# The running maximum of an mLSTM goes to all partitions by transfers instead of matmuls, and the order of a pass is changed

## The reference

```python
def mlstm(q, k, v):                      # one sequence, 8 heads of 64
    ig, fg = gates(concat(q, k, v))      # (8, 256) each
    cs = cumsum(log_sigmoid(fg))
    log_D = where(tril, cs[s] - cs[t] + ig[t], -inf)
    m = max(log_D, axis=t)
    C = (q @ k.T / 8) * exp(log_D - m)
    h = C / (max(|sum C|, exp(-m)) + 1e-6) @ v
    return layernorm(h) * ln_scale
x = x + tanh(g0) * mlstm(layernorm(x), ctx, ctx)
z = layernorm(x)
x = x + tanh(g1) * (top2_of_16_experts(z) + shared_expert(z))
```

## Time and the profile before

| what | value |
|---|---|
| median of three runs | 1074.41 us (1070.31 to 1075.37) |
| the profiled execution | 1070.1 us, of which 1068.5 us are the span from the first to the last instruction |
| busy share of the span | PE 90%, PEld 75%, DVE 76%, ACT 40%, POOL 39% |
| mean granted clock of TensorE | 0.956 of full speed |
| chain that ended last, by engine | PE 69%, DVE 13%, issue 7%, DMA 5%, POOL 4% |
| L1084 and L1086, all of the loop | 256 matmuls each, 48.9 and 44.7 us busy |

### The profile page before, as it was taken

One profiled execution on the slowest core, in us unless ns is written; L12 is line 12 of the kernel. 1 busy time (PEld: TensorE's weight loads), 2 busy tenths in 40 slices (PEclk: granted clock), 3 DMA queues, 4 the chain that ended last, 5 costly groups with the idle time before them and its releaser, 6 DMA issues.

```text
span 1068.5 us, 21065 instructions
## 1 busy us (share of the span) xinstructions
PE 959.1 (90%) x6143; PEld 804.3 (75%) x6143; DVE 807.3 (76%) x1995; ACT 424.7 (40%) x957; POOL 419.4 (39%) x315
## 2 busy tenths in 40 slices
PE   3689999999999998988998399999999999999982
PEld 2569888988898886977777278888888888677761
DVE  2887889888988989898866576666666666555885
ACT  2654445444544554444522134444444444332110
POOL 5010211221122122222123827668667777104775
PEclk9989999999999999999958699999999999999996
DMA  7570201220122022111004475576677674915888
GB/s 253 209 311 2 80 31 51 80 79 21 61 80 80 10 72 81 60 60 41 11 31 158 139 227 178 178 231 186 179 212 214 177 213 150 335 70 153 261 291 260
DMA packets 92778, 147.26 MB, mean 138 GB/s; under 512 B 10720, under 2 KB 51168, under 8 KB 91776
## 3 DMA queue, kind: packets, MB, share of 16 engines
q0 software_dynamic: 17872, 65.02, 18.8%
q1 hardware_dynamic: 62896, 59.79, 17.9%
q10 hardware_dynamic: 11904, 21.11, 5.6%
HBM read 89.26 MB, written 56.62 MB: 137 GB/s over the span
## 4 chain that ended last, share of the span: by engine, by line
PE 69%; DVE 13%; issue 7%; DMA 5%; POOL 4%; ACT 1%; SPq 1%; DVEq 0%; POOLq 0%; ACTq 0%
PE bank L1282 19%; PE bank L1152 13%; PE bank L1301 9%; PE bank L1165 5%; PE bank L1075 4%; POOL w_ring L699 3%; PE bank L1007 3%; PE bank L1096 2%; PE bank L1097 2%; PE bank L1349 2%; PE bank L1099 2%; DMA x2n<-routed_x 2%; PE bank L1292 2%; DMA base_out<-in_x_dram 2%; PE bank L1125 1%
## 5 line engine op out<-in xcount | busy, mean ns | idle before, releaser
L1282 PE MATMUL bank<-w_ring,x2nT 128*128 x948 | 254.3, 406 | 13.9 <-DVE x2nT L1864 13.6
L1282 PEld LDWEIGHTS bank<-w_ring,x2nT 128*128 128x128 f32 x948 | 173.8, 191 | 51.5 <-issue 15.8
L1152 PE MATMUL bank<-x2nT,w_ring 128*128 128x256 f32 x1152 | 149.8, 286 | 0.0
L580 POOL DMA_INDIRECT routed_x<-x2n,slot_u x64 | 65.8, 1029 | 204.4 <-DVE slot_u L1625 189.5
L1152 PEld LDWEIGHTS bank<-x2nT,w_ring 128*128 128x128 f32 x1152 | 142.3, 190 | 0.3
L1301 PE MATMUL bank<-w_ring,sh_actT 128*128 x474 | 121.2, 391 | 3.5 <-DVE sh_actT L1853 3.5
L1853 DVE TENSOR_TENSOR sh_actT<-bank,sh_actT 128x256 fp32r<-128x256 f32 x79 | 33.6, 425 | 108.9 <-ACT sh_actT L922 108.9
L1301 PEld LDWEIGHTS bank<-w_ring,sh_actT 128*128 128x128 f32 x474 | 88.8, 188 | 24.0 <-issue 4.6
L662 POOL TENSOR_TENSOR w_ring<-area,one 128x3072 fp32r<-128x3072 f32 x14 | 74.2, 5303 | 81.4 <-PE bank L1301 81.4
L699 POOL DMA_INDIRECT w_ring<-routed_y,y_slot x64 | 66.9, 1046 | 78.0 <-DMA routed_y<-cs_in 52.9
L665 POOL TENSOR_TENSOR w_ring<-area,w_ring 128x3072 fp32r<-128x3072 f32 x14 | 95.9, 6849 | 2.5 <-POOL w_ring L662 2.5
(11 more groups left out here) (224 smaller groups left out, 1959.1 us busy)
## 6 DMA issues: line engine op xcount, KB each, us to landing
x2n<-routed_x SPq DMA_DIRECT2D x316, 64.0 KB, 2.6
routed_y<-cs_in ACTq DMA_DIRECT2D x79, 256.0 KB, 3.3
base_out<-in_x_dram SPq DMA_DIRECT2D x16, 512.0 KB, 5.1
cs_in<-in_ctx_dram SPq DMA_DIRECT2D x16, 512.0 KB, 4.0
area<-n_L_ffn_expert_gate_dram POOLq DMA_DIRECT2D x16, 512.0 KB, 5.2
area<-in_L_ffn_expert_up_dram POOLq DMA_DIRECT2D x16, 512.0 KB, 6.9
area<-n_L_ffn_expert_down_dram POOLq DMA_DIRECT2D x16, 512.0 KB, 8.4
out_dram<-base_out SPq DMA_DIRECT2D x32, 256.0 KB, 3.8
```

The lines of the kernel that those rows point to most:

```text
L580: pool.indirect_dma_start(out=routed_x, in_=x2n[:, b.par, j, :], in_offset=None, out_offset=bass.IndirectOffsetOnAxis(ap=slot_u[:, b.par, ...
L1152: last = mm(gu_bank(b.n, m)[:, at:at + S], w[:, w_part, c, m * P:(m + 1) * P], x2nT[:, x_part, c, :], start=(c + p == 0), stop=(c == DC - ...
L1282: last = mm(bank[2 + t.par][:, :], xtT[:, x_part, t.par, c * P:(c + 1) * P], w_gu[:, bass.ds(slot, 1), w_part, c, :].rearrange("p a i -> p ...
```

## The change

- spread, its constants (identb, mask_b, head_sel), the bf16 parts of max_row and the banks MB go. Instead SP stores max_row to DRAM (max_store) and loads it back, two heads at a time, into all 128 partitions (max_load: the two rows whole, and their second halves once more). GpSimd writes the mask into the first copy (mask, one select of 128 x 512 elements for two heads). ScalarE's head reads the result from SBUF.
- max_spread has two buffers; the load of pair q waits until the decays of pair q - 2 are made.
- The banks that MB held become a second pair of score banks, so scores_pair runs one pair further ahead.
- GpSimd's order: two masks of A behind h_stats, then values, x2_stats, two masks of F, stats, and scatter last.
- VectorE: top and choose go behind turn(G, 0); rank behind turn(G, 1); stats, slots and weigh to other places behind rows_end. ScalarE: top goes behind turn(G, 0), ahead of heads 6 and 7. TensorE: rank behind turn(G, 1), scores_pair(A, 3) ahead of gates_sum.
- The zero rows are written in four pieces in steps t = 5 to 8, the kept weights in six pieces in steps t = 10 to 15.

```diff
-        TP, SM, MB, QK, HO, FF = bank[0], bank[1], bank[2:4], bank[4:6], bank[6], bank[7]
+        TP, SM, QK, HO, FF = bank[0], bank[1], (bank[4:6], bank[2:4]), bank[6], bank[7]
...
-        max_rest = sb("max_rest", [FG + NH, S])[FG:, :]
-        max_parts = sb("max_parts", [P, 2, S], BF16)
+        max_spread = sb("max_spread", [P, 2, 2 * ST + 2, P])
...
-        zeros = base_out[:, NT // 2, :]
+        zeros = base_out[:, NT - 1, :]
...
-        row_step = event("row_step", 8)
-        max_hi_made = event("max_hi_made")
+        row_step = event("row_step", 5)
+        max_out = event("max_out", 16)
+        max_in = [event(f"max_in{k}", 32) for k in range(2)]
+        max_masked = event("max_masked")
...
+            def max_store(b):
+                sp.wait_ge(row_step.sem, row_step.upto(b.n, 4))
+                sp.dma_start(max_rows[b.par], max_row[:, :]).then_inc(max_out.sem, 16)
+
+            def max_load(b, q):
+                k, lap = q % 2, b.n * 2 + q // 2
+                sp.wait_ge(max_out.sem, max_out.upto(b.n))
+                sp.wait_ge(decay_made.sem, decay_made.upto(b.n, 2 * q - 2))
+                two = max_rows[b.par, 2 * q:2 * q + 2, :]
+                sp.dma_start(max_spread[:, k, 0:2 * ST, :].rearrange("p (h j) n -> p h (j n)", h=2),
+                             two.partition_broadcast(P)).then_inc(max_in[k].sem, 16)
+                sp.dma_start(max_spread[:, k, 2 * ST:, :], two[:, P:S].partition_broadcast(P)
+                             ).then_inc(max_in[k].sem, 16)
+
+            def max_front(b):
+                max_store(b)
+                max_load(b, 0)
+                max_load(b, 1)
+
+            def max_back(b):
+                max_load(b, 2)
+                max_load(b, 3)
+
             load_next(Item(0, 2))
+            max_front(Item(0, 0))
+            max_back(Item(0, 0))
             load_next(Item(0, 3))
-            sp.wait_ge(zeros_made.sem, zeros_made.upto(0))
-            sp.dma_start(routed_x[0:DUMP, :].rearrange("(e r) d -> r e d", e=E)[0:P],
-                         zeros.unsqueeze(1).to_broadcast([P, E, D])).then_inc(padded.sem, 16)
-            sp.dma_start(routed_x[DUMP:DUMP + P, :], zeros).then_inc(padded.sem, 16)
+            max_front(Item(0, 1))
             sp.wait_ge(shared_in.sem, shared_in.upto(SHARED_PIECES - 1))
-            for part in range(2):
-                sp.dma_start(kept_w[part], sh_flat[:, part, :].bitcast(F32)).then_inc(kept_w_out.sem, 16)
+
+            def pad(k):
+                own = routed_x[0:DUMP, :].rearrange("(e r) d -> r e d", e=E)[0:P, k * PADS:(k + 1) * PADS]
+                sp.dma_start(own, zeros.unsqueeze(1).to_broadcast([P, PADS, D])).then_inc(padded.sem, 16)
+
+            def keep_w(k):
+                part, at = k // 3, slice(k % 3 * DC * IS, (k % 3 + 1) * DC * IS)
+                sp.dma_start(kept_w[part][:, at], sh_flat[:, part, at].bitcast(F32)).then_inc(kept_w_out.sem, 16)
             for b in range(4, B):
-                if b == B // 2 - 2:
-                    sp.wait_ge(padded.sem, padded.upto(1))
+                if b == B - 3:
+                    sp.wait_ge(padded.sem, padded.upto(E // PADS))
+                max_back(Item(0, b - 3))
                 load_next(Item(0, b), more=b + 2 < B)
+                if b == B // 2:
+                    sp.wait_ge(zeros_made.sem, zeros_made.upto(0))
+                    sp.dma_start(routed_x[DUMP:DUMP + P, :], zeros).then_inc(padded.sem, 16)
+                if B // 2 <= b < B // 2 + E // PADS:
+                    pad(b - B // 2)
+                max_front(Item(0, b - 2))
+                if b >= B - 3:
+                    keep_w(b - B + 3)
+            for b in range(B - 3, B):
+                max_back(Item(0, b))
+                if b + 1 < B:
+                    max_front(Item(0, b + 1))
+                keep_w(b - B + 6)
...
-                g.memset(zeros, 0.0).then_inc(zeros_made.sem, 1)
-                const(g.memset(identb[:], 0.0))
...
-                const(g.memset(mask_b[:], 0.0))
...
-                const(g.memset(max_parts[:], 0.0))
...
-                select(identb[:], 1.0, ALU.not_equal, 0, 1, [[-1, P]])
...
-                select(mask_b[:], MASK, ALU.is_ge, 0, -1, [[1, P]])
...
-                const(g.memset(head_sel[:], 0.0))
-                for part in range(3):
-                    select(head_sel[:], 1.0, ALU.not_equal, -FG * part, 1, [[-1, NH], [0, P]])
...
+            def mask(b, q):
+                k, lap = q % 2, b.n * 2 + q // 2
+                pool.wait_ge(max_in[k].sem, max_in[k].upto(lap))
+                own = max_spread[:, k, 0:2 * ST, :]
+                g.affine_select(out=own, in_=own, compare_op=ALU.is_ge, fill=MASK, base=0,
+                                pattern=[[0, 2 * ST], [1, P]], channel_multiplier=-1).then_inc(max_masked.sem, 1)
...
+                if attend:
+                    mask(A, 2)
+                    mask(A, 3)
+                if front:
+                    values(F)
                 if route:
                     x2_stats(G)
+                if front:
+                    mask(F, 0)
+                    mask(F, 1)
+                if ahead:
+                    stats(N)
                 if rest and route:
                     scatter(H)
-                if front:
-                    values(F)
-                if ahead:
-                    stats(N)
...
+                if t == 4:
+                    pool.wait_ge(shared_in.sem, shared_in.upto(SHARED_PIECES - 1))
+                    g.memset(zeros, 0.0).then_inc(zeros_made.sem, 1)
...
-            def max_hi(b):
-                act.wait_ge(row_step.sem, row_step.upto(b.n, 4))
-                act.wait_ge(max_spread.sem, max_spread.upto(b.n - 2))
-                s.copy(max_parts[0:NH, b.par, :], max_row[:, :]).then_inc(max_hi_made.sem, 1)
-
...
 
             def head(b, h):
                 act.wait_ge(key_made.sem, key_made.upto(b.n))
-                act.wait_ge(max_spread.sem, max_spread.upto(b.n, h + 1))
+                act.wait_ge(max_masked.sem, max_masked.upto(b.n * 4 + h // 2))
...
-                s.activation(decay[:, k, 0:S], MB[k][:, 0:S], ACT.Exp,
+                s.activation(decay[:, k, 0:S].rearrange("p (j n) -> p j n", j=ST),
+                             max_spread[:, h // 2 % 2, k * ST::2 * ST - k, :], ACT.Exp,
                              bias=key_log[:, b.par, 0, h:h + 1], scale=-1.0)
-                s.activation(decay[:, k, S:TRI], MB[k][:, S:TRI], ACT.Exp,
+                s.activation(decay[:, k, S:TRI], max_spread[:, h // 2 % 2, k * ST + 1, :], ACT.Exp,
...
-                if inner and route:
-                    top(H)
                 if front:
                     abs_gates(F)
                 if route:
                     turn(G, 0)
+                if inner and route:
+                    top(H)
...
-                    max_hi(F)
...
-                pe.wait_ge(c_made.sem, c_made.upto(b.n, 2 * q))
+                pe.wait_ge(c_made.sem, c_made.upto(b.n, 2 * q - 2))
                 for at, frm, n in ((0, 0, S), (S, P, P)):
                     for k in range(2):
                         half = slice(DH * k, DH * (k + 1))
-                        last = mm(QK[k][:, at:at + n], ctxT[half, b.par, q, frm:frm + P],
+                        last = mm(QK[q % 2][k][:, at:at + n], ctxT[half, b.par, q, frm:frm + P],
                                   xnT[half, b.par, q, S - n:S], start=True, stop=True)
                 last.then_inc(qk_made.sem, 1)
-
-            def spread(b, h):
-                k = h % 2
-                pe.wait_ge(row_step.sem, row_step.upto(b.n))
-                pe.wait_ge(decay_made.sem, decay_made.upto(b.n, h - 1))
-                for at, n in ((0, S), (S, P)):
-                    mm(MB[k][:, at:at + n], head_sel[0:3 * FG, h, :], max_parts[0:3 * FG, b.par, S - n:S],
-                       start=True, stop=False)
-                    last = mm(MB[k][:, at:at + P], identb[:, :], mask_b[:, :], start=False, stop=True)
-                last.then_inc(max_spread.sem, 1)
...
                     scores_pair(A, 0)
-                    spread(A, 0)
-                    spread(A, 1)
+                    scores_pair(A, 1)
                 if rest:
                     shared(H, 2)
                 if front:
                     turn_ctx(F, 0)
                 if attend:
-                    spread(A, 2)
-                    spread(A, 3)
                     pv(A, 0)
                     pv(A, 1)
-                    scores_pair(A, 1)
                 if front:
                     turn_ctx(F, 1)
                 if rest:
...
                 if front:
                     turn_x(F, 0)
                 if attend:
-                    spread(A, 4)
-                    spread(A, 5)
                     scores_pair(A, 2)
                 if front:
                     turn_x(F, 1)
...
                 if front:
                     gates_pe(F)
                 if attend:
-                    spread(A, 6)
```

(40 more changed lines are left out.)

35 lines of the change are left out of this document (15 added, 20 removed).

## The result

The changed kernel takes 1112.7 us (1111.7 to 1115.8), the kernel before in the same comparison 1074.9: a ratio of 1.0365 [1.0328, 1.0402]. It is 3.65% slower, where 1055 us were forecast. The profiled execution has a span of 1114.3 us, 45.8 more than the 1068.5 before. It is the slowest of the four runs of the changed kernel (1115.8 us), and the profile of before lies at the low end of its runs; the medians are 37.8 apart, so about 8 of the 45.8 us come from which executions were profiled.

What follows compares the result with a forecast made beforehand. TensorE (33.0 us a pass) and the loop through GpSimd (32.9) were to meet; with 0.6 for masks, 33.6. 1070.1 - 19.8 (steady) + 3 (late) + 0 = 1053, plus 2 for a low profiled run: 1055 us, range 1044 to 1078.

Steps and rivals of the forecast that it cites:

- TensorE's list: TensorE's own work in a steady pass: falls from 35.30 to 33.0 us as the spread matmuls leave.
- X to S: From x2_add's start (X) to the end of the scan making max_row (S): 17.9 us, hardly changed from 18.35.
- wait for the gap: ScalarE's gap_exp, ahead of heads 6 and 7, waits about 2 us for VectorE's gap, bringing S to X + 17.9.
- S to the next X: From the max_row scan's end to the next x2_add: 15.0 us, set by store, loads, masks, scatter and h_rstd.
- GpSimd's line: Chain behind S: store and loads, mask 1 (S + 7.8), rstd, scatter (13.6), h_rstd (14.3), next x2_add at S + 15.0.
- The clock: TensorE's granted clock: no term in the sum; its fall inside the steady passes was named as a sign of being wrong.
- Masks: GpSimd's masks holding up VectorE instructions with two SBUF inputs: one mask charged, 0.6 us a steady pass (0 to 2.5).
- third rival: Masks block VectorE at full price, 2.5 us a pass in place of 0.6: 1069 to 1071 us, no change; chance 0.15.
- The late passes: t = 10 to 15, where every other pass lacks the shared expert: +3 us together (0 to +8).
- the queue through scatter: GpSimd's masks, scatter and h_rstd ahead of x2_add in late passes: t = 11 and t = 13 each lose 2.6 us.
- The first passes: Head 0 of t = 0 comes about 2 us later while spreads and constants leave: 0 (-3 to +3).
- The rest: From the experts on, behind the sixteen passes, nothing is touched: 0.

Runs made afterwards that it cites:

- e1: Changed kernel with ScalarE's gap_exp moved from ahead of heads 6 and 7 to behind turn(G, 1): 1077.2 us, ratio 1.0032 to before.
- e3: e1 with VectorE's second shared_down sum also moved ahead of rows(F): 1092.4 us, ratio 1.0165 to before.
- e7: Changed kernel with twelve idle matmuls between the router and shared(G, 0) in the steady passes: 1102.6 us, ratio 1.0266 to before.
- e9: e5 with idle bf16 matmuls where TensorE waits in passes lacking half of a shared expert: 1060.0 us, ratio 0.9880 to before.
- e5: e1 with GpSimd's scatter moved ahead of masks 0 and 1 of the next sequence: 1073.2 us, ratio 0.9985 to before.
- e6: e1 without the running maximum's stores, loads and masks, max_spread filled once with a constant: 1056.4 us, ratio 0.9834 to before.
- e8: Changed kernel, order untouched, without the running maximum's stores, loads and masks (max_spread a constant): 1094.6 us, ratio 1.0193 to before.
- e4: Changed kernel's transfers, masks and bank pairs with the earlier kernel's order on VectorE, ScalarE and TensorE: 1092.6 us, ratio 1.0173 to before.
- e10: e5 with VectorE's second shared_down sum moved ahead of rows(F): 1083.6 us, ratio 1.0097 to before.

## Why the prediction was wrong

**TensorE's list** (33.0 us) was about right: 32.2 busy in e1's pass, though a few records can be missing.

**X to S** (17.9): the mechanism was right, the size 0.9 short. The wait for the gap is there (2.11 us); x2n came at X + 7.3 (6.9 forecast), the gap at X + 11.25 (10.8), ScalarE's turn(G, 1) ended at X + 15.65 (14.9). The failure is the sentence that closes this step, "what top's move saved ahead of x2n is given back here; X to S hardly changes". It names VectorE as the one who waits for turn(G, 1) and stops. TensorE's router waits for it too, and the sum behind rows makes shared(G, 0) wait for the same delay.

**S to the next X** is the step that failed: "So this loop is 17.9 + 15.0 = 32.9 us". The 15.0 was GpSimd's line, and the changed kernel's and e3's rows show that line where I put it. But in before this stretch took 17.7 us with no such line in it, so something else set it: VectorE's sum, then TensorE's shared(G, 0), pv, logits, shared(G, 1) and on, without a gap. I swapped the old line for the new instead of taking the longer of the two. e1 shows it at full clock: 17.0. The steady pass is then, from the rows: 32.9, +0.9 for X to S, +2.0 for S to X (17.0 for 15.0), +1.5 for the half clock (e7) = 37.3, as measured.

**The clock** had no term at all; the prediction names its fall in the steady passes only as a sign of being wrong. It cost 1.5 us in each of seven of the eight (not in t = 9), and e9's gain on e5 (13.2 us between medians, 17.3 between the profiled executions), all of it in t = 1, 11 and 13, goes with the clock as well. The prediction had t = 1 at nothing, and in the late passes it counted the spreads' going only as a gain of 0.4 us each; that the clock could fall there is not in it.

**Masks** (0.6 us, third rival up to 2.5): the size was about right (0.45 us of X to S) and the sum wrong, since it is hidden (e6). In the passes read it fell on the short norm_floor behind x2_add more than on x2_add itself: at 258.90 that kept its 1.40 us although a mask ran from 259.65 on, and the mask took 1.18 us where the one at 284.95 took 0.64. But one x2_add beside a mask took 1.78 us (296.19 in the changed kernel; 1.40 in every row shown of e6). By the rule of the Trainium skill (SBUF — State Buffer, Who interferes with whom) a VectorE instruction with two SBUF inputs contends with a GpSimd instruction that reads SBUF. This trace agrees in kind, by the 1.78 us. The contention did not set the time.

**The late passes** (+3): the queue through scatter was named and found. Three x2_adds of the changed kernel wait for h_rstd, 2.62 us in t = 11, 2.20 in t = 13, and 1.98 in t = 15, which the prediction had left out; taking the queue away gave 1.4 and 1.0 us in t = 10 and t = 12 (e5 against e1). Of the 24.0 us, e1 takes back 9.2 (the wait for the gap again), e5 2.8 more and e9 10.5 (the clock); 1.6 are left. These shares hold for this order of steps only: e6, with the transfers alone taken out of e1, already takes 16.2 us off, so the waits that the transfers bring and the clock that falls there are not told apart. Each of the six passes lacks a half of a shared expert, t = 10, 12 and 14 the first half and t = 11, 13 and 15 the second; it is not only every other one.

**The first passes** (0): ahead of X of t = 1 the transfers cost 5.4 to 7.3 us, not 2, since sequence 0 has no earlier pass to hide them. Head 0 of sequence 0 and head 0 of sequence 1 in the changed kernel, and the first of them in e8:

```profile
36.24 0.51 ACT L824 ACTIVATE area<-max_spread,key_log 128x256 f32<-128x256 f32 x1 [4.52 <-POOL max_spread L608]
...
68.09 0.51 ACT L824 ACTIVATE area<-max_spread,key_log 128x256 f32<-128x256 f32 x1 [2.08 <-POOL max_spread L608]
```

```profile
31.55 0.49 ACT L828 ACTIVATE area<-max_spread,key_log 128x256 f32<-128x256 f32 x1
```

Head 0 waits 4.52 us for mask 0 and begins 4.7 us later than in e8, and head 0 of sequence 1 waits 2.08 us again. The second pair of loads costs nothing: head 4 comes 9.4 us behind head 0 in both kernels. The other 4.4 us lie in t = 1, where the granted clock is 0.74 (0.95 in before), and e9 takes more than that off by raising it to 1.00. Why TensorE idles there is open: t = 1 takes 34.1 us in e8 and in e4, but 37.6 in e6.

**The rest** (0): +2.2 us behind the sixteen passes, e5 and e9 about the same; no run separated it.

With gap_exp late, scatter first and the clock kept up (e9), the chip gives -19.0 us in the eight steady passes and +1.6 in the late ones, where the prediction had -19.8 and +3. It had priced the change without what its order does to TensorE. The agreement in the steady pass (33.7 for 33.6) is partly luck: the halves are 16.7 and 17.0, not 17.9 and 15. What is left of that pass above TensorE's 32.3 us busy (e5) are the wait for the sum (0.7) and one for xn (0.7); e10 removed the first without a gain, so what sets the pass at 33.7 stays open.

## What to carry to other kernels

When a change puts a new line of work across a stretch, the stretch takes the longer of the new line and the old one: find what set it before, and keep that in the sum until something shortens it. When an instruction is delayed, follow every engine that waits for what it makes, and price TensorE's idle time twice, once as a wait and once as the slower matmuls that can come after it. Small matmuls that look like pure cost may be what keeps the clock up in a thin pass; before taking them off TensorE, see what else it has to do there.

## What the runs showed of the hardware that was not expected

In seven of the eight steady passes of the changed kernel, waits of some 0.6 and 1.82 us with 1.2 us of matmuls between them were followed by a lower granted clock (in t = 6 0.62 over the next 4 us, shared(G, 0) 4.52 us in place of 3.1). In the eighth, t = 9, the same waits were not (3.10 us, clock 1.00); why, no run shows. Matmuls whose result nobody reads kept the clock up: twelve in each steady pass (e7, 1.00 in all eight), or about 90 of 0.06 us each in a thin one (e9; in t = 11 0.50 to 0.63 before, 0.85 to 1.00 with them).
